# Moving small VectorE steps of a cross-attention and mixture-of-experts kernel to ScalarE and GpSimd, scattering one tick earlier, and re-timing its paddings and down weights

## The reference, cut to what matters

```python
x = x + xattn(layernorm(x), ctx, mask)      # x: 64 sequences x 128 tokens x 512 features
x = x + moe(layernorm(x), G, gate_w, up_w, down_w, lora_A, lora_B)

def xattn(h, ctx, mask):                    # ctx: 64 x 128 x 512, one head as wide as D
    s = h @ ctx.T / sqrt(512); s[~mask] = -1e30
    return softmax(s) @ ctx                 # zero where a sequence's mask is empty

def moe(x, ...):                            # 8 experts, the 2 best of each token, expert width 64
    scores = softmax(x @ G)                 # weights: the two best scores, not renormalised
    out  = sum_e w[e] * (silu(x @ gate[e].T) * (x @ up[e].T)) @ down[e].T
    out += sum_e w[e] * (x @ lora_A[e].T) @ lora_B[e].T      # rank 16
```

## Time and profile before

| what | value |
|---|---|
| median of three runs | 526.15 us |
| the profiled execution | 524.49 us, its span 522.4 us |
| busy over the span | PE 95%, PEld 84%, DVE 85%, ACT 71%, POOL 56% |
| DMA | 189.10 MB, mean 362 GB/s; 61.3% and 32.8% of the 16 engines by SyncE's and GpSimd's queues |
| chain that ended last | PE 82%, issue 4%, DVE 2%, POOL 2% |

### The profile page before, as it was taken

One profiled execution on the slowest core, in us unless ns is written; L12 is line 12 of the kernel. 1 busy time (PEld: TensorE's weight loads), 2 busy tenths in 40 slices (PEclk: granted clock), 3 DMA queues, 4 the chain that ended last, 5 costly groups with the idle time before them and its releaser, 6 DMA issues.

```text
span 522.4 us, 16239 instructions
## 1 busy us (share of the span) xinstructions
PE 495.9 (95%) x4040; PEld 437.5 (84%) x4040; DVE 445.6 (85%) x1758; ACT 369.0 (71%) x1012; POOL 293.3 (56%) x423
## 2 busy tenths in 40 slices
PE   8999999999999998697999999999999999999994
PEld 7787888888888886586888899889999999999883
DVE  5899999999999996576888899898888888888675
ACT  4777888787787887566788778777566666666452
POOL 4227677676778776743885454444545454445434
PEclk9999999999999999989999999999999999999988
DMA  8999999999999999999997999979999999999722
GB/s 311 394 328 324 405 408 404 396 401 385 407 405 397 403 317 316 399 343 375 313 376 272 390 389 388 333 302 386 418 413 415 414 417 416 415 415 414 308 85 81
DMA packets 65607, 189.10 MB, mean 362 GB/s; under 512 B 9582, under 2 KB 9710, under 8 KB 65520
## 3 DMA queue, kind: packets, MB, share of 16 engines
q1 hardware_dynamic: 44352, 120.20, 61.3%
q0 software_dynamic: 20800, 67.65, 32.8%
q10 hardware_dynamic: 368, 0.22, 0.2%
HBM read 114.04 MB, written 78.73 MB: 369 GB/s over the span
## 4 chain that ended last, share of the span: by engine, by line
PE 82%; issue 4%; DVE 2%; POOL 2%; ACT 1%; another core or an unknown queue 1%; POOLq 0%; ACTq 0%
PE bank L528 13%; PE rd L528 13%; PE bank L470 11%; PE bank L372 9%; PE rd L546 7%; PE rd L547 6%; PE rd L412 5%; PE rd L413 4%; PE bank L351 4%; PE rd L385 4%; PE rd L535 3%; PE rd L392 1%; PE bank L405 1%; PE bank L368 1%; POOL out_x L1222 1%
## 5 line engine op out<-in xcount | busy, mean ns | idle before, releaser
L654 ACT COPY hT<-bank 128x512 f32<-128x512 f32 x140 | 81.7, 583 | 30.2 <-PE bank L470 17.1
L1207 POOL DMA_INDIRECT x_rows<-xe x64 | 64.9, 1014 | 41.4 <-DVE xe L816 22.7
L528 PE MATMUL rd<-wg_sb,hT 128*128 x560 | 82.3, 291 | 1.0 <-issue 1.0
L528 PE MATMUL bank<-wg_sb,hT 128*128 x560 | 80.4, 287 | 1.0 <-issue 1.0
L372 PE MATMUL bank<-cc_sb,xnT 128*128 128x136 f32 x512 | 80.1, 286 | 0.0
L528 PEld LDWEIGHTS rd<-wg_sb,hT 128*128 128x128 f32 x560 | 74.5, 194 | 1.3 <-issue 1.2
L528 PEld LDWEIGHTS bank<-wg_sb,hT 128*128 128x128 f32 x560 | 72.6, 190 | 1.5 <-issue 1.4
L546 PE MATMUL rd<-dn_a,ggT_a 128*128 x140 | 67.7, 484 | 1.9 <-issue 0.8
L372 PEld LDWEIGHTS bank<-cc_sb,xnT 128*128 128x128 f32 x512 | 68.4, 191 | 0.3
L1222 POOL DMA_INDIRECT out_x<-z_shared x41 | 39.9, 972 | 42.5 <-issue 37.3
L1108 DVE SCALAR_TENSOR_TENSOR z_shared<-rd,z_shared 128x512 f32<-128x512 f32 x77 | 57.7, 749 | 1.9 <-PE rd L547 0.2
(11 more groups left out here) (186 smaller groups left out, 1196.9 us busy)
## 6 DMA issues: line engine op xcount, KB each, us to landing
cc_sb<-in_cc SPq DMA_DIRECT2D x64, 532.0 KB
z_shared<-z_rows SPq DMA_DIRECT2D x41, 516.0 KB
x_sb<-in_x SPq DMA_DIRECT2D x64, 256.0 KB
z_own<-z_rows SPq DMA_DIRECT2D x29, 516.0 KB
z_shared<-x_rows SPq DMA_DIRECT2D x36, 260.0 KB
z_own<-x_rows SPq DMA_DIRECT2D x34, 260.0 KB
z_rows<-pad SPq DMA_DIRECT2D x8, 516.0 KB
wg_sb<-in_wg SPq DMA_DIRECT2D x8, 288.0 KB
```

The costliest lines, as they stand in the source:

```text
L528: mm = pe.matmul(gu_ps[q % 2][:, 0:GU], hT[:, q % 2, k, :], wg_flat[:, bass.ds(at + k * GU, GU)], start=(k == 0), stop=(k == KD - 1))
L654: act.copy(hT[:, q % 2, :, :], hT_ps[q % 2][:].rearrange("p (k s) -> p k s", k=KD)).then_inc(hT_ready, 1)
L1207: pool.indirect_dma_start(out=x1_rows[:, :], out_offset=rows_at(row, ROW1), in_=row, in_offset=None, bounds_check=ROWS - 1, oob_is_err=Fal ...
```

## The change

- **Scatters at tick n + 9.** GpSimd scatters tile t-9 in tick t, not t-10. After the sweep one scatter less is left, and tiles 60 to 63 go out after blocks 5, 8, 11 and 14, not 2, 5, 8 and 11.
- **Routing part on ScalarE.** keep_part moves from VectorE to ScalarE, behind keep_pT. VectorE's mask_scores(n) now also waits for keep_part(n).
- **Row numbers on GpSimd.** number(m) moves from VectorE to GpSimd, at tick 4m + 8.
- **Paddings at tiles 6 to 11**, by the list PADDED_AT, not at 10 to 52.
- **Copied down weights.** An odd part of the down weights is the even one but for its last 32 rows. Those alone are loaded (64 KB for 256 KB, from a new input), and ScalarE copies the other 96 rows from the finished even part (down_same) in place of down_left. down_hi of an odd part works on 32 partitions. The zeros that the sum then needs are set once by GpSimd.
- **Sums at ticks 57 and 61**, not 58 and 62, with the loads and ScalarE's parts that belong to them.
- The last batch is weighed at tick 7 of the second stage (WEIGHED), not 5.

```diff
-SUMS_AT = sorted([*range(TB * 2 + 3, B, TB), B - 6, B - 2])
+SUMS_AT = sorted([*range(TB * 2 + 3, B, TB), B - 7, B - 3])
+PADDED_AT = [6, 7, 8, 8, 9, 9, 10, 11]
-RANKED, SHARED, COUNTED, SUMMED, TABLE, OVERLAP, SKIP = 2, 5, 7, 21, 25, 26, 30
+RANKED, SHARED, WEIGHED, COUNTED, SUMMED, TABLE, OVERLAP, SKIP = 2, 5, 7, 7, 21, 25, 26, 30
 # SyncE
-                if n % 6 == 4 and (n - 10) // 6 in range(E):
+                for i in range(E):
+                    if n == PADDED_AT[i]:
...
+                    if i % 2 == 0:
+                        sp.dma_start(dn_part(i).bitcast(F32), dn[:, i // 2, :]).then_inc(dn_loaded, 16)
+                    else:
+                        sp.dma_start(dn_part(i)[KG:P, :].bitcast(F32), dn_rest[:, i // 2, :]).then_inc(dn_loaded, 16)
 # ScalarE
+            def down_same(i):
+                act.wait_ge(dn_ready, i)
+                act.copy(dn_part(i)[0:KG, :], dn_part(i - 1)[0:KG, :].bitcast(F32)).then_inc(dn_low_left, 1)
+            def keep_part(n):
+                m, b = divmod(n, TB)
+                act.wait_ge(scores_done, n + 1)
+                act.activation(x_sb[:, n % RX, D:D + E], sc_ps[:, S:S + E], ACT.Copy, scale=std1[:, m % 2, b:b + 1]).then_inc(part_ready, 1)
...
                 if in_sweep(t, 2):
                     keep_pT(t - 2)
+                if in_sweep(t, 1):
+                    keep_part(t - 1)
 # VectorE
             def mask_scores(n):
                 dve.wait_ge(scores_done, n + 1)
+                dve.wait_ge(part_ready, n + 1)
-                    keep_part(t - 1)
-                    number((t - 9) // TB)
 # GpSimd
+            pool.memset(dn_hi[:, 1, :], 0.0).then_inc(dn_hi_set, 1)
-                if in_sweep(t, 10):
+                if in_sweep(t, 9):
                     pool.wait_ge(x1_ready, min(t - 2, B))
-                    scatter_x1(t - 10)
+                    scatter_x1(t - 9)
+                if in_sweep(t, 8) and (t - 8) % TB == 0:
+                    number((t - 8) // TB)
...
-                if q % 3 == 2 and q // 3 in range(TB):
-                    scatter_x1(B - TB + q // 3)
+                if q % 3 == 2 and q // 3 - 1 in range(TB):
+                    scatter_x1(B - TB + q // 3 - 1)
```

More of the change, by code:

```diff
@@ L95, with xattn_moe @@
 NCONST = PACK + len(GROUPS)
-def xattn_moe(nc, x, cc, mask, wg, dn, g, consts, out):
+def xattn_moe(nc, x, cc, mask, wg, dn, dn_rest, g, consts, out):
     with ExitStack() as stack:
@@ L224, in dn_part, with down_rows @@
             return (dn_a, dn_b)[i % 2][:, i // 2, 0:D]
+        def down_rows(i):
+            return slice(0, P) if i % 2 == 0 else slice(KG, P)
         def left(q, ring):
@@ L623, in down_hi @@
                     act.wait_ge(dn_ready, i - 1)
-                act.activation(dn_hi[:, i % 2, :].bitcast(F32R), dn_part(i).bitcast(F32), ACT.Copy, scale=const_sb[:, SIGN:SIGN + 1]).then_inc(dn_hi_ready, 1)
+                if i == 1:
+                    act.wait_ge(dn_hi_set, 1)
+                own = down_rows(i)
+                act.activation(dn_hi[own, i % 2, :].bitcast(F32R), dn_part(i)[own, :].bitcast(F32), ACT.Copy, scale=const_sb[own, SIGN:SIGN + 1]).then_inc(dn_hi_ready, 1)
+            def down_same(i):
+                act.wait_ge(dn_ready, i)
+                act.copy(dn_part(i)[0:KG, :], dn_part(i - 1)[0:KG, :].bitcast(F32)).then_inc(dn_low_left, 1)
             def down_left(i):
@@ L678, in _ @@
                 if t in SUMS_AT:
-                    down_left(SUMS_AT.index(t))
+                    i = SUMS_AT.index(t)
+                    if i % 2 == 0:
+                        down_left(i)
+                    else:
+                        down_same(i)
                 if in_sweep(t, 0):
@@ L718, in _ @@
                     normalise(later)
-                if t == SHARED - 1:
+                if t == WEIGHED - 1:
                     router_exp(NB - 1)
@@ L795, in mask_scores @@
                                          rowmin[:, n % 2, :]).then_inc(masked_ready, 1)
-            def keep_part(n):
-                m, b = divmod(n, TB)
-                dve.tensor_scalar(x_sb[:, n % RX, D:D + E], sc_ps[:, S:S + E], std1[:, m % 2, b:b + 1], None, ALU.mult).then_inc(part_ready, 1)
             def row_weights(n):
@@ L891, in weigh_row @@
                                          op0=ALU.mult, op1=ALU.mult).then_inc(weight_ready, 1)
-            def number(m):
-                dve.tensor_scalar(xe[:, slots_of(m), TOKEN].bitcast(I32), const_sb[:, IDS:IDS + TB], float(TB * P * m), None, ALU.add).then_inc(token_ready, 1)
             def centre_g():
@@ L1122, in _ @@
                     locate_row(NB - 1)
-                if t == SHARED:
+                if t == WEIGHED:
                     weigh_sum(NB - 1)
-                    number(NB - 1)
                     weigh_inverse(NB - 1)
@@ L1178, in norms, with number @@
                 pool.tensor_tensor(xe[:, own, SHIFT], neg[:, 1, :], xe[:, own, RSTD], ALU.mult).then_inc(norm_step, 1)
+            def number(m):
+                own = slice(TB * m % RE, TB * m % RE + TB)
+                pool.tensor_scalar(xe[:, own, TOKEN].bitcast(I32), const_sb[:, IDS:IDS + TB], float(TB * P * m), None, ALU.add).then_inc(token_ready, 1)
             def gaps(m):
@@ L1371, in _ @@
                     early_table()
-            for n in range(SWEEP - 10, B - TB):
+            for n in range(SWEEP - 9, B - TB):
                 scatter_x1(n)
             norms(NB - 1)
+            number(NB - 1)
             gaps(NB - 1)
@@ L1429 @@
     down, lora_b = down.transpose(2, 0, 1), lora_b.transpose(2, 0, 1)
-    back = np.stack([np.concatenate([down[:Q], lora_b, lora_b, down[Q:], again], 0) for again in (down[:Q], down[Q:])], 1)
+    back = np.concatenate([down[:Q], lora_b, lora_b, down[Q:], down[:Q]], 0)
     consts = np.zeros((P, NCONST), np.float32)
@@ L1450 @@
         consts[j * GP:j * GP + E, at:at + E] = np.eye(E)
-    arrays = {"x": x, "cc": cc, "mask": mask, "wg": into, "dn": back, "g": g, "consts": consts}
+    arrays = {"x": x, "cc": cc, "mask": mask, "wg": into, "dn": back, "dn_rest": down[Q:], "g": g, "consts": consts}
     arrays = {f"in_{n}": np.ascontiguousarray(a) for n, a in arrays.items()}
```

13 lines of the change are left out of this document (7 added, 6 removed).

## The result

The changed kernel takes 516.91 us, the median of 4 runs (516.27 to 517.79), beside 526.17 us for the kernel before (525.43 to 526.51, 4 runs on the same chip). The ratio is 0.9827, with a 95% interval of 0.9809 to 0.9845: 9.3 us or 1.7% faster. 517.6 was predicted, in a range of 512 to 526.5. The profiled execution took 516.81 us, with a span of 515.0, against 524.49 and 522.4 before.

A forecast was written before the change was run, and what follows sets the result against it. VectorE and TensorE together were taken to pace the sweep, TensorE alone the second stage. The terms -5.2 - 2.5 + 0.5 - 1.3 = -8.5 us on 524.49 gave 516.0, or 517.6 us as a median; range 512 to 526.5.

The forecast's parts named there:

- What bounds the kernel: Whole kernel: VectorE and TensorE together pace the sweep, TensorE the second stage; gains before that stage stay to the end.
- Period of four ticks: Steady sweep: from 12.35 to 12.0 us a period, a gain of 0.35, times 15 makes -5.2 us.
- TensorE keeps the pace: Rival for the sweep: the scatter pair stays as harmful, the period stays 12.35 us; 524 us in all, chance 0.20.
- pair of scatters: Sweep: two GpSimd scatters 1.33 us apart hold up TensorE's signals; at about 1.7 us half of TensorE's wait goes.
- The reading of the mask: VectorE's mask in the sweep: scores are done 0.3 to 1 us early in three of four ticks, hiding keep_part.
- slower rival: ScalarE in line with the mask: VectorE waits for keep_part, deciding above 0.6 us a period; 530 us, chance 0.17.
- the prediction's own test: Sweep: the reading of bursts is wrong if pairs stay 1.33 us apart and the stalls vanish, or the reverse.
- Sums at 57 and 61: Late sweep: three scatters in a row come apart into a pair and one, sparing VectorE's stall; -2.5 us.
- the +0.5 for ScalarE: Ticks 55, 57, 59 and 61: ScalarE has both down_hi and a copy, 0.71 us more in each; +0.5 us counted.
- The last scatters: Sweep's end: one of six scatters in a run is gone, norms and late signals come 1.28 us sooner; -1.3 us.
- The places of the late tiles: Second stage: tiles 60 to 63 still stand between the blocks, four as before; 0.
- DMA edits: Loads: copied down weights save 1.6 MB but VectorE never waits for loads, 0; paddings at tiles 6 to 11, 0.

The follow-up runs named there:

- first group: Follow-up runs on one chip, each with one edit to the kernel before, which took 506.66 us there.
- third group: The changed kernel again (517.97 us, 0.9861) and with single parts taken out, on one chip; the kernel before took 524.92 us there.
- second and third group: Two sets of follow-up runs, parts added to the kernel before or variants of the changed one; the kernel before took 523.55 and 524.92 us.

## Why the prediction was right, and where it was not

**What bounds the kernel: right for the passage, half right for the sweep.** The sweep gave 3 of the 7.4 us of the span and the passage up to block 10 the other 4.4, and from there on nothing was lost, as forecast. In the sweep VectorE was held to be the bound once the stalls were gone. It isn't: it is busy 95% now, and TensorE 99%.

**Period of four ticks: mis-sized, -0.35 predicted, -0.2 measured.** The saving on VectorE (0.14 a tick, keep_part at 0.27 on ScalarE) was right to the hundredth. The term that was mis-sized is TensorE's: "by TensorE at 12.35 - 0.4 (3.0 us over the 7.3 periods of rows 7) = 11.95 without the stall". The 3.0 us are waits of the weight loads, which overlap the matmuls. The matmuls themselves had only 1.41 us of idle time in these 90 us, 0.19 a period, so TensorE's own work is 12.37 - 0.19 = 12.18 us a period, and the forecast of 12.0 lay below it. The changed kernel takes 12.17, with TensorE idle for 0.05 us in 90. In the 24 steps behind the first 20 TensorE is busy for 12.1 to 12.3 us a period in all fourteen traces. The rival "TensorE keeps the pace" had the right engine, though not for its reason, the pair of scatters.

The reading of the mask was wrong too. "In three of four ticks the scores are done 0.3 to 1 us before VectorE comes to the mask": from 60 to 150 us of the trace before this holds for two ticks of four; in the other two the mask starts within 0.1 us of the scores' end in 12 of 15 cases. The slower rival named this mechanism and the point from which it decides, 0.6; the waits stopped at 0.39, two thirds of that, over several ticks and not one. Over the sweep the term gives 3.0 us in place of 5.2.

**The pair of scatters: outcome right, reason not held up.** The strips' wait was to be halved and went altogether, at a distance of 2.38 and not 1.7. But a new pair 1.35 us apart stands one tick on, and in the first group the old pair, 1.33 us apart, does no harm at all. By the prediction's own test ("wrong if the pairs stay 1.33 us apart and the stalls vanish") the reading that a burst by itself holds up TensorE's signals is wrong. Where signals do come late, the table above shows it for the runs at the sweep's end. For the pair it is likely but not shown: the three kernels there that keep the old order of the scatters have 4.6 to 6.5 us of waits for the strips from 60 to 150 us, all others 0.4 or none, but no run changed the distance alone. With the tick undone the pair is 1.62 us apart and the strips wait 0.4 us, far less than the half that was counted at 1.7. And the stall was worth little: the two kernels there without it and with the part on VectorE take 73.9 us for 24 steps, against 74.2.

**Sums at 57 and 61: the stall went, the time did not.** There is no stall of 3 us near tick 61, as forecast. The last 19 steps of the sweep took 59.7 us (152.3 to 212.0) and now take 59.1 (149.8 to 208.9): 0.6 us where -2.5 + 0.5 = -2.0 was predicted. With the part back on VectorE (third group) they take 58.6. So the term was some -1.0 in place of -2.5, since waits of 1.8 and 1.0 us for late scores remain in the place of the old one, and the +0.5 for ScalarE was about right. Moved alone, the sums gave nothing in the first group, which has no stalls; where there are stalls they weren't tried alone.

**The last scatters: under-sized, -1.3 predicted, about -2 measured.** With the tick undone block 0 comes 1.9 us later, and from the kernel before to the one after it comes 2.0 us sooner behind the last add_readout (11.0 to 9.0). The prediction counted one scatter less, 1.28 us, and took the norms and the late signals behind it to come just so much sooner. The 3.6 us between the medians aren't this term alone: in the traces 1.4 us come with the lower clock.

**The places of the late tiles: costed at 0, 2.3 us measured** up to block 5 in the traces (1.5 in the medians, at the edge of no change). This is the term that the prediction put at nothing. Its reason was that the tiles still stand between the blocks, four as before. What it left out is that the scatter behind block 2 has a stall behind it, by its own reading of the late signals. The whole change takes block 8 from 34.1 to 28.2 us behind the last add_readout (246.1 - 212.0, 237.1 - 208.9): 2.0 at block 0, 1.7 because the lower clock comes later, given back but for 0.2 by block 10, and 2.3 at block 5.

**DMA edits: 0, right.** Between 20 and 42 us the queues moved 395 GB/s where 336 were before; the first add_readouts come no later (15.0 against 14.9), and without the edits the ratio is the same. The reason given, that VectorE never waits for a load, holds with the part on VectorE only: with it on ScalarE and the loads as they were VectorE waits 1.7 to 1.9 us for them from 60 to 150 us (two traces). That fits the prediction's remark that a shorter tick would ask for more than the queues move.

**The sum.** -8.5 on the profiled execution became -7.7 (524.49 to 516.81). Of it 3.1 come from the sweep, where 7.2 were counted (-5.2 - 2.5 + 0.5), and the other 4.6 from the passage, where 1.3 were. Two errors, of 4.1 and 3.3 us, nearly cancel. That the number was met is luck in part; the sign stood on firmer ground, since the new wait was priced and stayed, from 60 to 150 us, below the point where it decides.

**Left open.** The parts measured in the second and third group (3.6 for the tick, 1.3 for the routing part, up to 1.5 for the places, 0 for the DMA edits) make 6.4 of the 7.0 us between the medians of the third; the intervals are too wide to say that nothing is left, and the share of the clock in the 3.6 belongs to no part for certain. What makes TensorE's signals late in some groups and not in others isn't settled, nor whether it is the chip, nor why the blocks behind block 10 take 5.1 us less where the kernel before takes 507. Whether the whole change gains where the kernel before takes 507 us wasn't tried; three of its parts gained nothing there.

## What to carry to other kernels

Before a gain is forecast for one of two engines that are both nearly full, add up what the other one is busy for in a period: that is the floor. Here TensorE's matmuls filled 12.18 us of 12.37, and 0.6 us off VectorE's list gave 0.2. Idle time has to be that of the matmuls; the waits of the weight loads, which overlap them, were twice as long. Where two stages meet, look for an engine that empties its own queue first (here GpSimd with six scatters at 1.28 us): one item less there moved the next stage by more than the item. Compare milestones in pairs before a loss is said to grow: one stretch of 3.4 us at the lower clock made 1.4 us of a difference that looked like a growing one. And time the parts of a change beside each other: the same kernel differed by 4% from one group to the next, and what a part was worth may differ with it.

## What the runs showed of the hardware

- The kernel before took 526.17, 506.66, 523.55 and 524.92 us in four groups of runs. In the one of 506.66 us no wait of ScalarE for the strips is left from 60 to 150 us (the kernel before with its sums moved), with the same 1.33 us between the scatters that stood beside 6.5 us of such waits in the first.
- In the groups of 524 to 526 us the second tanh of the second stage came 0.04 us behind its matmuls with no run of scatters around it, 0.04 to 1.4 with four in a row and 3.6 to 3.9 with five or six. In the group of 506.66 us it came 0.04 us behind them with four, five or six.
- TensorE's granted clock fell to 1.2 GHz for 3.4 us at a time. With the tick undone this was from 219.5 to 222.9 us, after TensorE had stood still from 215 to 218 us and run again from 218.1; there two blocks took 5.3 us and not 3.9.
- Indirect scatters issued by GpSimd mostly start 1.27 to 1.36 us apart in a row (0.97 to 1.06 us each and 0.30 of idle time). Behind a small operation of its own the idle time was 0.97 us in the changed kernel (109.97) and 0.27 with the tick undone (109.75). A scatter that waited for VectorE's add_readout started 0.80 us behind its end (113.15 in the kernel before).
- With the mask waiting for keep_part on ScalarE it started at least 0.42 us behind the end of the scores, and 0.04 us behind it where it waited for them alone.
- A `tensor_scalar` of 128x8 with a busy time of 0.22 us cost VectorE 0.14 us of its list, as the statistics behind the mask start that much sooner without it.
